# Two attentions: three unread products of 128 rows by 512 columns behind every block of values

## Chip, cores and metric
One core of one Trainium2 chip runs the whole program. The metric is the device time of one execution in microseconds (us), the median of several runs. Lower is better.

## What is computed
Input x has shape (8, 512, 128). Two layers, each an attention and a feed-forward part, each with a residual and a layer norm over the last axis behind it:

```python
x = layernorm(x + attn0(x))   # 16 heads of 8, rotary, causal softmax, output projection
x = layernorm(x + moe(x))     # top 2 of 7 experts, and a shared one
x = layernorm(x + attn1(x))   # 16 heads of 8, rotary, softmax over all keys, no projection
x = layernorm(x + dense(x))   # ternary weights, 128 -> 512 -> 512 -> 512 -> 128
```

The three products of the change feed none of this.

## The kernel before
The function `attention` runs twice, first with the causal mask ("causal attention"), then without ("full attention"). x lies in SBUF in tiles of 128 tokens. Work goes by batch b (8) and, in it, by group of four heads t (4); n = 4b + t counts the 32 groups. A group is cut into units u: 12 in causal attention (three tiles of scores, shortened by the mask, times four heads), 16 in full attention.

The order on each engine is written out by hand. On TensorE the loop over n and u does, in each unit:

- `scores(n, u)`: keys by queries for one head. q and k are split into a high and a low part and stacked as 24 rows of a 32-row quadrant, in fp32r; a 25th row of q subtracts the row's maximum. So the stationary operand has 25 rows by 128 columns. Result to one of three banks ps_s; ScalarE takes the exponential into `prob` (L430).
- `maxima(n+2, u)`: queries by keys, 24 rows, two groups ahead, to one of three banks ps_m; VectorE reduces each to row maxima (L575 causal, L578 full).
- `values`, in some units only (the map `sh.values`): a block j of 128 keys, four heads side by side in the columns of the array, 128x32 each, fp32 (each product is two records in the trace), accumulating in bank ps_o. In causal attention block 0 comes at unit 8, blocks 1, 3 and 2 at units 0, 1 and 4 of the next group; in full attention blocks 0, 1, 2 come at units 6, 10, 14 and block 3 at unit 2 of the next group.
- `job`, in some units: small work through the one bank ps_x (XB = 1), each with a stationary operand of 128x128: `maxT` (maxima transposed, every group), `norm` (outputs transposed for the division, every group), and once per batch `xT`, `k`, `q`, `v`, and in causal attention `yT` and `proj`. A job waits until the job before it has been read out of the bank (semaphores `s_read`): ScalarE reads most, VectorE reads norm and proj.

SyncE (SP) issues the transfers. `stack(b)` copies the high and low parts of k and q of a batch into `kst` and `qst` by 24 DMAs; `max_row(n)` moves the row of maxima of group n into `qst`. Both stand in one queue: in each batch, stack(b+1) is issued between the rows of its second and third groups. The first scores of a group wait for its row. The lines that move a row and wait for it:

```python
for n in range(G):
    if n + 1 < G:
        max_row(n + 1)
    if n % NG == 0 and n // NG + 1 < B:
        stack(n // NG + 1)
```

GpSimd does the rotary arithmetic and hides the masked part of the diagonal blocks (`hide`).

Of the kernel before, what the change touches and what calls it, by code (L numbers as in the profile page):

```python
# [11 lines left out]
P = 128  # L12
# [6 lines left out]
NG = H // HG  # L19
# [110 lines left out]
def after(eng, sem, count):  # L130

    if count > 0:
        eng.wait_ge(sem, count)
# [98 lines left out]
def attention(nc, sems, x, x_dram, ident, maskw, weights, wproj, cos, sin, tag, ahead=None):  # L232
# [4 lines left out]
    U = sh.units  # L237
    G = B * NG
    SB, MB, XB = 3, 3, 1
    START = [("xT", 0), ("k", 0), ("q", 0), ("v", 0), ("xT", 1), ("k", 1), ("q", 1), ("maxT", 0)]  # L240
    END = [("norm", G - 1)] + ([("yT", B - 1), ("proj", B - 1)] if causal else [])
    place = sh.ring(START, END, XB)

    with ExitStack() as ctx:
        def psum(name, shape, dt=F32):
            return ctx.enter_context(nc.psum_tensor(tag + name, shape, dt))

        def sbuf(name, shape, dt=F32):
            return ctx.enter_context(nc.sbuf_tensor(tag + name, shape, dt))
# [3 lines left out]
        kst = [sbuf(f"kst{r}", [P, NG, T], F32R) for r in range(2)]  # L253
# [22 lines left out]
        ps_j = [psum(f"ps_x{i}", [P, T]) for i in range(XB)]  # L276
# [4 lines left out]
        s_made, s_read, s_swap, s_turn, s_hi, s_lo = sems.made, sems.read, sems.swap, sems.turn, sems.hi, sems.lo  # L281
# [3 lines left out]
        def stacked(b):  # L285

            return (b // 2 + 1) * STACK

        with nc.Block() as block:
# [63 lines left out]
            def _(pool):  # L353
# [9 lines left out]
                def hide(n, j):  # L363

                    k, (col, _) = sh.tile_of[j], sh.piece_of[j]
                    pool.wait_ge(s_exp, n * U + (k + 1) * HG)
                    diag = prob[k][:, :, col:col + P]
                    pool.affine_select(out=diag, in_=diag, compare_op=ALU.is_ge, fill=0.0, base=0,  # L368
                                       pattern=[[0, HG], [1, P]], channel_multiplier=-1).then_inc(s_mask, 1)
# [20 lines left out]
            def _(act):  # L390
# [48 lines left out]

                for name, n in START:  # L440
                    read_out(name, n)
# [11 lines left out]

            @block.tensor
            def _(pe):
                def job(name, n):

                    slot, before = place[name, n]
                    ps_x = ps_j[slot]
                    if before is not None:  # L460
                        pe.wait_ge(s_read[before[0]], before[1] + 1)
                    if name == "xT":
                        if causal:
                            pe.wait_ge(s_load[n], 16)
                        for i in range(QT):
                            last = pe.transpose(ps_x[:, P * i:P * i + P], x[:, QT * n + i, :], ident[:, :])
                    elif name in "kq":
                        pe.wait_ge(s_read["xT"], n + 1)
                        last = pe.matmul(ps_x[:, :], weights[name][:, :], xT[:, :], start=True, stop=True)
                    elif name == "v":  # L470
                        for i in range(QT):
                            last = pe.matmul(ps_x[:, P * i:P * i + P], xT[:, P * i:P * i + P], weights["v"][:, :],
                                             start=True, stop=True)
                    elif name == "maxT":
                        pe.wait_ge(s_mx, (n + 1) * U)
                        last = pe.transpose(ps_x[:, 0:P], mx[n % 2][:, :], ident[:, :])
                    elif name == "norm":
                        pe.wait_ge(s_oT, n + 1)
                        for i in range(QT):
                            last = pe.transpose(ps_x[:, P * i:P * i + P], oT[:, P * i:P * i + P], ident[:, :])  # L480
                    elif name == "yT":
                        pe.wait_ge(s_read["norm"], (n + 1) * NG)
                        for i in range(QT):
                            last = pe.transpose(ps_x[:, P * i:P * i + P], y[:, i, :], ident[:, :])
                    else:
                        assert name == "proj"
                        pe.wait_ge(s_read["yT"], n + 1)
                        for i in range(QT):
                            last = pe.matmul(ps_x[:, P * i:P * i + P], yT[:, P * i:P * i + P], wproj[:, :],
                                             start=True, stop=True)  # L490
                    last.then_inc(s_made[name], 1)

                def scores(n, u):

                    b, t = divmod(n, NG)
                    r, (k, i), g = b % 2, divmod(u, HG), n * U + u
                    if u == 0:
                        pe.wait_ge(s_mst, (n + 1) * 16)
                    after(pe, s_exp, g - SB + 1)
                    lo_row, end = QUAD * i, QUAD * i + KROWS + 1  # L500
                    for j, col, w in sh.score[k]:
                        last = pe.matmul(ps_s[g % SB][:, col:col + w], kst[r][lo_row:end, t, P * j:P * j + P],  # L502
                                         qst[r][lo_row:end, t, T - w:T], start=True, stop=True)
                    last.then_inc(s_score, 1)

                def maxima(n, u):

                    b, t = divmod(n, NG)
                    r, (k, i), g = b % 2, divmod(u, HG), n * U + u
                    if u == 0 and t == 0:  # L510
                        pe.wait_ge(s_kst[r], stacked(b))
                        pe.wait_ge(s_qst[r], stacked(b))
                    i = (i + 2) % HG
                    after(pe, s_mx, g - MB + 1)
                    lo_row, end = QUAD * i, QUAD * i + KROWS
                    for j, col, w in sh.maxima[k]:
                        last = pe.matmul(ps_m[g % MB][:, col:col + w], qst[r][lo_row:end, t, P * j:P * j + P],  # L517
                                         kst[r][lo_row:end, t, 0:w], start=True, stop=True)
                    last.then_inc(s_max, 1)

                def values(n, j):

                    b, t = divmod(n, NG)
                    k, (col, w) = sh.tile_of[j], sh.piece_of[j]
                    if causal:
                        pe.wait_ge(s_mask, sh.values_done(n, j))
                    else:
                        pe.wait_ge(s_exp, n * U + (k + 1) * HG)
                    if j == 0:
                        after(pe, s_oT, n)  # L530
                        if t == 0:
                            pe.wait_ge(s_read["v"], b + 1)
                    for i in range(HG):
                        last = pe.matmul(ps_o[VW * i:VW * i + VW, T - w:T], vst[b % 2][:, j, HG * t + i, :],  # L534
                                         prob[k][:, i, col:col + w], start=(j == 0), stop=(j == sh.order[-1]))
                    last.then_inc(s_pv, 1)

                for name, n in START[:-1]:
                    job(name, n)
                for u in range(U):  # L540
                    maxima(0, u)
                for u in range(U):
                    maxima(1, u)
                    if u == 3:
                        job("maxT", 0)
                for n in range(G):
                    for u in range(U):
                        scores(n, u)
                        if n + 2 < G:
                            maxima(n + 2, u)  # L550
                        for back, j in sh.values.get(u, []):
                            if n >= back:
                                values(n - back, j)
                        for name, m in sh.jobs(n, u):
                            job(name, m)
                for j in [j for u in sorted(sh.values) for back, j in sh.values[u] if back]:
                    values(G - 1, j)
                for name, n in END:
                    job(name, n)
# [1457 lines left out]
```

## Time and profile before

| | us |
|---|---|
| median of 3 runs | 1616.12 |
| lowest, highest | 1610.1, 1623.22 |
| the profiled execution | 1627.57 |
| its span, first to last instruction | 1625.9 |
| TensorE busy | 1321.6 |
| VectorE busy | 927.4 |
| ScalarE busy | 795.7 |
| GpSimd busy | 520.5 |

The mean granted clock of TensorE over the span is 0.753 (1 is 2.4 GHz, 0.5 is 1.2 GHz). PE is TensorE's matmul part, PEld its weight loads, DVE VectorE, ACT ScalarE, POOL GpSimd, SP SyncE. Matmul records overlap, since a product goes through the array while the next one starts; so the distance from start to start tells what one costs, and its recorded duration is longer.

### The profile page before, as it was taken

Reading aid. Unit: us, or ns where it says so; the run is one execution under the profiler, and the core shown is the slowest. Engines: PE = TensorE matmul, PEld = TensorE weight load, DVE = VectorE, ACT = ScalarE, POOL = GpSimd, SP = SyncE. Lnnn points to the kernel's source line nnn. Section 1 sums busy time; section 2 is a strip of 40 time slices with the busy share of each in tenths; the row PEclk is TensorE's granted clock in tenths of the full one; section 3 lists DMA queues with packets and bytes.
Section 4 is the critical chain, followed back from the end, with each engine's and each line's share of the span. In section 5 each row is a group of like instructions: output and inputs, shape, how many; then the busy total and the mean of one; then the engine's idle time right before and its main releaser. Section 6 shows DMA issues by size and latency. Waiting matters only on the chain. (4 is left out here: it accounts for less than half of the span.)

```text
span 1625.9 us, 21073 instructions
## 1 busy us (share of the span) xinstructions
PE 1321.6 (81%) x6651; PEld 681.9 (42%) x6651; DVE 927.4 (57%) x2838; ACT 795.7 (49%) x1543; POOL 520.5 (32%) x476
## 2 busy tenths in 40 slices
PE   3678977788898586983589888888888867999997
PEld 1334333333333454761223223233232216888885
DVE  3546665675563774547557777777686513343443
ACT  1234444554444662533146656557565434655653
POOL 3314423551411465654203113113030002554453
PEclk9966576875556698995557778778585557999998
DMA  4212112211200402431321121120220000000000
GB/s 98 35 22 41 19 23 40 40 19 23 40 2 1 127 7 63 109 66 34 80 56 24 17 40 18 23 40 16 26 41 1 1 0 20 1 26 13 13 19 14
DMA packets 55918, 52.77 MB, mean 32 GB/s; under 512 B 8000, under 2 KB 38720, under 8 KB 55824
## 3 DMA queue, kind: packets, MB, share of 16 engines
q1 hardware_dynamic: 51808, 48.33, 15.4%
q0 software_dynamic: 3696, 2.76, 1.3%
q8 instruction: 47, 0.77, 0.2%
q14 instruction: 47, 0.39, 0.1%
q10 hardware_dynamic: 320, 0.52, 0.1%
HBM read 15.74 MB, written 8.06 MB: 15 GB/s over the span
## 5 line engine op out<-in xcount | busy, mean ns | idle before, releaser
L430 ACT ACTIVATE a_prob<-a_ps_s 128x512 f32<-128x512 f32 (+1 forms) x896 | 472.3, 568 | 461.2 <-PE a_ps_s L502 458.9
L578 DVE TENSOR_REDUCE a_mx<-a_ps_m 128x1 f32<-128x512 f32 x512 | 329.3, 684 | 156.0 <-PE a_ps_m L517 154.6
L517 PE MATMUL a_ps_m<-a_kst,a_qst 24*128 24x512 f32 (+3 forms) x1024 | 379.5, 577 | 46.4 <-DMA a_qst<-a_lo_q 36.9
L502 PE MATMUL a_ps_s<-a_qst,a_kst 25*128 25x512 f32 (+3 forms) x1024 | 359.7, 572 | 49.5 <-DMA a_qst<-a_mrow 34.3
L534 PE MATMUL a_ps_o<-a_prob,a_vst 128*32 128x512 f32 (+3 forms) x2048 | 339.6, 749 | 2.2 <-POOL a_prob L368 1.4
L575 DVE CUSTOM_DVE_ANT_0 a_junk<-a_ps_m,maskw 128x384 f32<-128x384 f32 (+3 forms) x512 | 230.1, 487 | 188.0 <-PE a_ps_m L517 186.0
L502 PEld LDWEIGHTS a_ps_s<-a_qst,a_kst 25*128 25x128 f32 x1024 | 158.8, 247 | 404.9 <-ACT a_prob L430 207.2
L517 PEld LDWEIGHTS a_ps_m<-a_kst,a_qst 24*128 24x128 f32 x1024 | 169.8, 246 | 77.9 <-issue 40.5
L368 POOL TENSOR_SCALAR_AFFINE_SELECT a_prob<-a_prob 128x512 f32<-128x512 f32 x128 | 79.7, 635 | 308.7 <-ACT a_prob L430 308.4
L335 POOL TENSOR_TENSOR a_rot_k<-a_rot_k,sin_table 128x512 f32<-128x512 f32 x16 | 20.4, 1272 | 313.4 <-DVE a_rot_k L586 313.4
L480 PE MATMUL a_ps_x<-ident,a_oT 128*128 128x128 f32 x256 | 60.5, 382 | 70.4 <-ACT a_oT L438 48.4
L1676 POOL TENSOR_TENSOR f_hid_lo<-f_gelu_h,f_hid_hi 128x512 fp32r<-128x512 f32 x64 | 83.1, 1299 | 101.8 <-ACT f_hid_hi L1639 101.8
L1714 PE MATMUL f_ps_h<-f_hid_hi,f_h_hi 128*128 128x512 f32 x256 | 103.5, 404 | 4.5 <-POOL f_hid_lo L1676 4.5
L1676 POOL TENSOR_TENSOR f_hid_lo<-f_gated_h,f_hid_hi 128x512 fp32r<-128x512 f32 x32 | 41.4, 1295 | 193.2 <-ACT f_hid_hi L1628 192.5
L1716 PE MATMUL f_ps_h<-f_hid_lo,f_h_hi 128*128 128x512 f32 x256 | 101.4, 396 | 0.0
L1715 PE MATMUL f_ps_h<-f_hid_hi,f_h_lo 128*128 128x512 f32 x256 | 100.7, 393 | 0.0
L534 PEld LDWEIGHTS a_ps_o<-a_prob,a_vst 128*32 128x32 f32 x2048 | 47.2, 127 | 83.3 <-issue 53.4
L480 PEld LDWEIGHTS a_ps_x<-ident,a_oT 128*128 128x128 f32 x256 | 39.5, 191 | 92.7 <-issue 65.8
L1714 PEld LDWEIGHTS f_ps_h<-f_hid_hi,f_h_hi 128*128 128x128 f32 x256 | 48.8, 191 | 16.1 <-POOL f_hid_lo L1676 6.7
L1811 DVE SCALAR_TENSOR_TENSOR f_u<-f_th,f_ps_a 128x512 f32<-128x512 f32 x32 | 21.9, 683 | 56.0 <-ACT f_th L1623 56.0
L1716 PEld LDWEIGHTS f_ps_h<-f_hid_lo,f_h_hi 128*128 128x128 f32 x256 | 48.6, 190 | 11.2
L1715 PEld LDWEIGHTS f_ps_h<-f_hid_hi,f_h_lo 128*128 128x128 f32 x256 | 48.8, 191 | 10.1
(290 smaller groups left out, 1885.3 us busy)
## 6 DMA issues: line engine op xcount, KB each, us to landing
a_kst<-a_hi_k SPq DMA_DIRECT2D x128, 64.0 KB
a_qst<-a_hi_q SPq DMA_DIRECT2D x128, 64.0 KB
f_w<-in_L_ffn_W_dram SPq DMA_DIRECT2D x21, 256.0 KB, 3.5
a_kst<-a_lo_k SPq DMA_DIRECT2D x64, 64.0 KB
a_qst<-a_lo_q SPq DMA_DIRECT2D x64, 64.0 KB
x_tiles<-in_L_attn_x_dram SPq DMA_DIRECT2D x8, 256.0 KB, 4.8
normed_rows_dram<-f_nrm SPq DMA_DIRECT2D x8, 256.0 KB, 2.3
f_hT_hi<-expert_sums_dram SPq DMA_DIRECT2D x4, 512.0 KB, 6.0
```

Source lines behind the costliest of these rows:

```text
L368: pool.affine_select(out=diag, in_=diag, compare_op=ALU.is_ge, fill=0.0, base=0, pattern=[[0, HG], [1, P]], channel_multiplier=-1).then_in ...
L430: act.activation(prob[k][:, i, 0:w], ps_s[g % SB][:, 0:w], ACT.Exp, scale=float(D) ** -0.5)\
L480: last = pe.transpose(ps_x[:, P * i:P * i + P], oT[:, P * i:P * i + P], ident[:, :])
L502: last = pe.matmul(ps_s[g % SB][:, col:col + w], kst[r][lo_row:end, t, P * j:P * j + P], qst[r][lo_row:end, t, T - w:T], start=True, stop= ...
L517: last = pe.matmul(ps_m[g % MB][:, col:col + w], qst[r][lo_row:end, t, P * j:P * j + P], kst[r][lo_row:end, t, 0:w], start=True, stop=True)
L534: last = pe.matmul(ps_o[VW * i:VW * i + VW, T - w:T], vst[b % 2][:, j, HG * t + i, :], prob[k][:, i, col:col + w], start=(j == 0), stop=(j ...
L575: ins = dve.tensor_tensor_reduce(junk[g % MB][:, col:col + w], bank[:, col:col + w], maskw[:, T - w:T], 1.0, -3.0e38, ALU.add, ALU.max, out)
L578: ins = dve.reduce_max(out, bank[:, col:col + w], AX.X)
L1676: pool.tensor_tensor(dst, src[:, :], hi.bitcast(F32), ALU.subtract).then_inc(s_lo, 1)
L1714: pe.matmul(out, w_hi[w][:, k, cols], hi, start=start, stop=False)
L1715: pe.matmul(out, w_lo[w][:, k, cols], hi, start=False, stop=False)
L1716: return pe.matmul(out, w_hi[w][:, k, cols], lo, start=False, stop=stop)
```

## The change
Behind every block of values, also where a group has no values yet, TensorE does three products of a 128x128 piece of `kst` with 512 columns of `kst`, fp32r, into bank ps_x. Nobody reads them. Ahead of each three it waits until the last job in ps_x has been read.

```diff
@@ -237,6 +237,7 @@
     SB, MB, XB = 3, 3, 1
+    WARM = 3
@@ -453,9 +454,20 @@
             @block.tensor
             def _(pe):
+
+                held = [None] * XB
+
+                def warm(r, t):
+
+                    if held[0] is not None:
+                        pe.wait_ge(s_read[held[0][0]], held[0][1] + 1)
+                    for _ in range(WARM):
+                        pe.matmul(ps_j[0][:, :], kst[r][:, t, 0:P], kst[r][:, t, :], start=True, stop=True)
+
                 def job(name, n):
 
                     slot, before = place[name, n]
+                    held[slot] = (name, n)
                     ps_x = ps_j[slot]
@@ -551,6 +563,7 @@
                         for back, j in sh.values.get(u, []):
                             if n >= back:
                                 values(n - back, j)
+                            warm(n // NG % 2, n % NG)
                         for name, m in sh.jobs(n, u):
                             job(name, m)
```

## Rows read from the trace of the kernel before

**Rows 1.** The page: TensorE's busy time, and its granted clock in 40 slices.
```profile
PE 1321.6 (81%) x6651; PEld 681.9 (42%) x6651; DVE 927.4 (57%) x2838; ACT 795.7 (49%) x1543; POOL 520.5 (32%) x476
PEclk9966576875556698995557778778585557999998
```

**Rows 2.** Windows over causal and full attention; the first row names the columns.
```profile
core 0: us, PE busy (x) PEld busy (x) DVE busy (x) ACT busy (x) POOL busy (x), PEclk, DMA share, GB/s
66.81:521.50 454.69, 380.85 (x2358) 169.88 (x2356) 263.67 (x1230) 220.41 (x478) 154.10 (x188) 0.66 0.17 26
...
808.74:1330.80 522.06, 455.20 (x2266) 150.21 (x2266) 349.04 (x750) 303.89 (x598) 75.82 (x60) 0.68 0.16 26
```

**Rows 3.** Windows over single groups: two of full, two of causal attention.
```profile
990.13:1002.67 12.54, 10.86 (x73) 3.63 (x71) 11.26 (x23) 9.67 (x20) 8.10 (x7) 1.00 0.01 2
1257.45:1276.17 18.72, 16.46 (x69) 4.99 (x69) 12.72 (x35) 9.12 (x19) 0.00 (x0) 0.50 0.01 2
232.89:241.98 9.09, 7.49 (x67) 3.51 (x63) 7.97 (x37) 6.84 (x17) 6.20 (x8) 1.00 0.01 2
...
216.45:232.89 16.44, 15.28 (x84) 5.91 (x83) 9.74 (x47) 7.47 (x16) 2.17 (x4) 0.54 0.01 1
```

**Rows 4.** Windows over batches: causal first and last, full fifth and last.
```profile
66.81:127.46 60.65, 50.49 (x269) 22.32 (x271) 31.33 (x139) 26.93 (x59) 14.73 (x20) 0.72 0.20 27
...
470.13:521.50 51.37, 46.71 (x277) 19.90 (x277) 21.14 (x98) 25.82 (x56) 10.27 (x17) 0.57 0.00 1
...
1064.47:1126.81 62.34, 53.83 (x293) 18.59 (x293) 46.97 (x103) 38.65 (x78) 12.62 (x11) 0.75 0.17 27
...
1257.45:1330.80 73.35, 62.74 (x239) 18.06 (x239) 25.97 (x67) 35.75 (x71) 0.00 (x0) 0.50 0.00 1
```

**Rows 5.** Windows in full attention: ahead of a rise, behind it, without one.
```profile
979.30:986.10 6.80, 6.80 (x33) 1.96 (x32) 4.32 (x8) 3.75 (x7) 0.00 (x0) 0.50 0.00 0
986.10:1006.60 20.50, 17.29 (x114) 5.67 (x110) 17.65 (x32) 15.59 (x32) 11.72 (x10) 1.00 0.01 2
1225.00:1305.00 80.00, 70.61 (x288) 21.55 (x288) 43.68 (x96) 38.48 (x77) 0.00 (x0) 0.50 0.00 1
```

**Rows 6.** Two of these windows, products to ps_x alone (PE busy, PEclk, DMA).
```profile
979.30:986.10 6.80, 1.16 (x5) 0.50 0.00 0
...
1225.00:1305.00 80.00, 7.22 (x24) 0.50 0.00 1
```

**Rows 7.** Waits of PE in full attention, longest total first (us, times, longest).
```profile
PE a_ps_x L480 <- ACT a_oT L438: 38.6, 31, 1.3
PE a_ps_s L502 <- ACT a_prob L430: 10.8, 34, 0.7
PE a_ps_x L476 <- DVE a_mx L578: 9.9, 28, 0.5
```

**Rows 8.** Timeline of full attention at full clock (start, us, engine, line).
```profile
1119.05 1.07 PE L534 MATMUL a_ps_o<-a_prob,a_vst 128*32 128x512 f32 x8
...
1120.05 0.49 PE L502 MATMUL a_ps_s<-a_qst,a_kst 25*128 25x512 f32 x1
...
1120.08 0.29 DVE L598 TENSOR_TENSOR a_y<-a_ps_x,a_rden 128x128 f32<-128x128 f32 x1
...
1120.48 1.12 PE L469 MATMUL a_ps_x<-a_xT,heads_q 128*128 128x512 f32 x2
...
1121.54 0.49 PE L502 MATMUL a_ps_s<-a_qst,a_kst 25*128 25x512 f32 x1
```

**Rows 9.** A window over the dense stage.
```profile
1400.00:1600.00 200.00, 200.00 (x900) 163.34 (x899) 90.43 (x237) 113.66 (x171) 99.81 (x77) 1.00 0.05 15
```

**Rows 10.** Timelines of SP and of PE: a stack and the row behind it.
```profile
246.23 5.67 SPq L302 DMA_DIRECT2D a_kst<-a_hi_k  x8
...
263.36 0.56 SPq L314 DMA_DIRECT2D a_qst<-a_mrow  x1
...
271.35 0.79 PE L502 MATMUL a_ps_s<-a_qst,a_kst 25*128 25x512 f32 x1 [6.12 <-DMA a_qst<-a_mrow]
```

## The prediction
> **What bounds the kernel now.** I first read the page's busy shares and its line of granted clock [rows 1]: TensorE is busy 81% of the span, and its clock stands near full only in the expert and dense stages, between 5 and 8 tenths in both attentions. The windows over the stages [rows 2] give the sizes: causal attention 454.69 us at a mean clock of 0.66, full attention 522.06 us at 0.68, together 60% of the span. The clock has two levels, 1.2 and 2.4 GHz, so 0.68 means some 64% of the time at the lower one.
>
> What a level is worth is seen in windows over one group of four heads [rows 3]. In full attention a group takes 12.54 us at clock 1.00 and 18.72 us at 0.50; in causal attention 9.09 us at 1.00, and 16.44 us at 0.54. So at the low level TensorE sets the pace; at the high one it shares it with VectorE, busy 11.26 of 12.54 us.
>
> Then what comes ahead of a rise. From 1225 to 1305 us the clock stays at 0.50 while TensorE is busy 70.61 of 80 us; its longest wait in full attention is 1.3 us [rows 5, 7]. Busy time alone does not raise the clock. What the rows show ahead of the rise at 986.1 is 6.8 us of unbroken work in which jobs with a stationary operand of 128x128 take 1.16 us (17%) beside the values; in the 80 us without a rise such jobs take 7.22 (9%) [rows 6]. Scores and maxima use 24 or 25 of the array's 128 rows, and a values product 32 of its columns; xT, k, q, v and norm use all of it. Every rise that I followed in full attention comes behind a stretch with one of the big jobs, and the last batch, which has none, is cold for all of its 73.35 us [rows 4].
>
> **The change part by part.** It adds 12 products of 128x128 by 512 columns to each group: 4 lumps of 3, 128 lumps in each attention. It removes nothing and adds one wait per lump.
>
> *Price of a lump.* Such products in fp32r run in the dense stage 900 in 200 us, 0.222 us each at full clock, weight loads hidden [rows 9]. Three take 0.67 us. A full-array job in attention pays something on top when the array goes over to another shape: q, two records in fp32, takes from 1120.48 to 1121.54 [rows 8], 1.06 us where four passes of 0.222 make 0.89, so 0.17. A lump stands right behind values, whose own changeover it may share. Bounds 0.67 and 0.84; I take 0.74, nearer the lower end because values also use all rows. Cold, a lump costs about twice that, 1.4.
>
> *The wait.* Ahead of a lump TensorE waits until the last job in the bank has been read. Queued behind it are the next scores and maxima, for which ScalarE and VectorE wait. It bites at one lump per group: behind values of block 0, where norm was the last job. The values end at 1120.05, VectorE's second read of norm at 1120.37 [rows 8]: 0.3 us. In the other lumps the job is two units or more old.
>
> *Clock.* A lump puts some 0.7 us (warm) or 1.4 us (cold) of full-array work behind every block of values, every 3 to 4 us of warm time, which in any such stretch is more than the 1.16 us of jobs that stood ahead of a rise [rows 6]. I therefore expect full attention at 0.97 to 1.00 from its second group on, and causal attention near 0.9, low only around its waits for DMA.
>
> *Full attention.* A batch of 62.34 us at 0.75 is half cold [rows 4]: 31.2/18.72 groups cold, the other 2.33 in 31.2 us, 13.4 us each; a plain warm group is 12.54. I take 12.9, so 32 groups make 413, less 3 for the last two, which have no maxima: 410, a gain of 112. Against it 128 lumps of 0.74 are 95 and 32 waits of 0.3 are 10, less 20 for places where TensorE now waits for VectorE or ScalarE anyway and a lump takes up the wait, plus 3 for a cold start: 88. Net -24.
>
> *Causal attention.* Here a fixed time hides some lumps. SyncE issues the 24 DMAs of a stack from 246.23 to 263.3, then the row of maxima; TensorE sat idle 6.12 us for that row until 271.35 [rows 10]: 25.1 us that no product moves. Six lumps (4.4 us) fall into it and are absorbed. Ten of each batch's 16 are exposed: 7.4, and 0.5 of waits. The group behind the wait takes 16.44 us at 0.54 [rows 3]; at full clock it would be near 9.9 (the 9.09 of the fourth group, and 0.8 for its longer jobs), and as it starts cold I put it at 11.9 without lumps, -4.5. A warm batch of 55.2 us (25.1 + 30.1) becomes 30.1 - 4.5 + 7.9 + 25.1 = 58.6. The first six batches take 344.7 now (60.65 the first; the eight make up the stage), so six of 58.6 are +7. The last two, with few big jobs, take 109.9 at 0.56 to 0.57 (51.37 the last [rows 4]); I put them at 99, -11. Net -4.
>
> *Sum.* -28 on the profiled execution: 1627.57 - 28 = 1600. That execution was 11.5 us above the median and 4 above the slowest of the timed runs. Part is the profile, part the luck of where the clock falls, which the change should take away; I take off about 9 for it: **1590 us**. The expert and dense stages are not touched.
>
> The Trainium skill ("TensorE: Matmul & The Clock Gate", section "HAM oscillation — how this bites in real kernels") ties the clock to idle gaps between bursts and advises keeping the array supplied. By that rule full attention, with no gap over 1.3 us, would be at full clock already and the lumps would be pure cost. The trace disagrees (0.50 for 80 us at 88% busy); the rule's outcome is the first rival.
>
> **The rivals.** *A: the clock does not follow the lumps.* Then each is work at the present mix: 128 lumps at 0.64 x 1.4 + 0.36 x 0.74 = 1.16 make 149 us, and some 80 exposed in causal attention 93: about 1865. For it: the clock's cause is only inferred. Against it: the rises behind jobs of the same kind. The skill's rule just named would give this. Chance 0.07.
>
> *B: the lump is dearer than it looks (slower).* If the 128-column weight load, 163.34 us for 899 or 0.18 us each in the dense stage [rows 9], is not hidden as it is there, each product costs 0.40 and a lump with its changeover some 1.25. Exposed are 128 + 70 lumps. The gain of 28 is gone at 0.74 + 28/198 = 0.88; at 1.25 the change costs 101 - 28 = 73: 1663. For it: operand and weights come from one tile and each lump stands between two shapes. Against it: in the dense stage loads hide one by one. Chance 0.11 for a time over 1632.
>
> *C: it cancels.* A lump at 0.84 gives +20 on my sum, or the group behind the DMA wait stays cold and pays its lumps at 1.4: +20. About 1612. Chance 0.25.
>
> *D: more is absorbed.* VectorE's slack in full attention hides lumps and the clock is full in causal attention too: -25 more, 1565. It belongs to my side; with the forecast itself 0.57.
>
> **How the numbers follow.** Two timings of this kernel within 1% cannot be told from no change. Faster by over 1% (under 1600) is forecast and D, 0.57; within 1% C, 0.25; slower A and B, 0.18. The range runs from below D, 1550, to 1640, past C and into B; left out are A, most of B and a little below: about 0.2.
>
> **What the profile will show.** Right: granted clock above 0.95 in full attention, the last batch no longer at 0.50, groups of about 15.5 us and almost alike; lumps starting 0.22 to 0.24 us apart; the wait for the row of maxima shorter than 6 us but the 25 us from the first DMA of a stack unchanged; the third group of a causal batch below 16 us. Wrong: a clock as before (A), more than 0.3 us between products or 0.9 us from a lump to the next scores (B), a causal group behind the DMA wait still at 0.5 (C). The forecast is most sensitive to the lump: 0.1 us on it is 20 us of time.

## The result and the profile after

The change makes the kernel slower: median 1688.54 us (1679.31 to 1691.43, 4 runs) against 1619.67 us (4 runs of before, three of them those of the table above), ratio 1.0425 with a 95% interval of 1.0351 to 1.0499. The forecast was 1590 us, range 1550 to 1640. The profiled execution took 1679.31 us, span 1677.6 us, which is 51.7 us over the span of before.

The page of the kernel after, its line of engine shares and its granted clock in 40 slices, against [rows 1]:

```profile
PE 1355.9 (81%) x7419; PEld 743.0 (44%) x7419; DVE 927.6 (55%) x2838; ACT 797.2 (48%) x1543; POOL 521.2 (31%) x476
PEclk9999999979978698895599999999999977999999
```

The clock line does what was forecast: nearly all nines in both attentions. TensorE has 768 more records and is not idler than before. The windows, against [rows 2] (causal, full) and [rows 3] (a fourth group of full attention, a fourth and a third of causal):

```profile
core 0: us, PE busy (x) PEld busy (x) DVE busy (x) ACT busy (x) POOL busy (x), PEclk, DMA share, GB/s
66.73:548.43 481.70, 411.19 (x2726) 198.62 (x2729) 265.71 (x1230) 220.68 (x477) 154.07 (x187) 0.92 0.16 24
836.89:1383.43 546.54, 459.70 (x2650) 182.33 (x2650) 349.12 (x750) 304.78 (x599) 75.95 (x60) 0.95 0.16 25
956.21:972.86 16.65, 13.79 (x83) 5.27 (x83) 11.81 (x23) 9.70 (x20) 8.84 (x8) 1.00 0.01 1
231.58:244.75 13.17, 11.21 (x83) 5.31 (x83) 8.54 (x37) 7.00 (x16) 7.19 (x8) 1.00 0.00 1
...
215.80:231.58 15.78, 14.32 (x96) 6.25 (x95) 9.64 (x47) 7.40 (x16) 2.17 (x4) 0.90 0.01 2
```

Read them by pairs. The clock of full attention went from 0.68 to 0.95, that of causal attention from 0.66 to 0.92; yet both became longer. Full attention runs from its first to its last exponential in 546.5 us instead of 522.1. The causal windows of before and after do not end at the same point, so I compare first to last exponential there too: 481.7 us against 453.0 (the start of the last one was at 519.82 before). So +24.5 and +28.7. The fast group shows why: at clock 1.00 both times, 16.65 us instead of 12.54, and in causal attention 13.17 instead of 9.09. Four lumps, with the waits ahead of them, cost 4.1 us a group, where my sum had 2.7.

Two lumps of full attention in the timeline (start, us, engine, line), to be set beside [rows 8]:

```profile
940.59 1.07 PE L546 MATMUL a_ps_o<-a_prob,a_vst 128*32 128x512 f32 x8
...
941.59 0.97 PE L465 MATMUL a_ps_x<-a_kst 128*128 128x512 f32 x3
942.48 0.50 PE L514 MATMUL a_ps_s<-a_qst,a_kst 25*128 25x512 f32 x1
...
945.24 1.06 PE L546 MATMUL a_ps_o<-a_prob,a_vst 128*32 128x512 f32 x8
...
946.26 0.29 DVE L611 TENSOR_TENSOR a_y<-a_ps_x,a_rden 128x128 f32<-128x128 f32 x1
...
946.61 0.97 PE L465 MATMUL a_ps_x<-a_kst 128*128 128x512 f32 x3 [0.31 <-DVE a_y L611]
947.51 0.49 PE L514 MATMUL a_ps_s<-a_qst,a_kst 25*128 25x512 f32 x1
```

From the start of a lump to the next scores it is 0.89 to 0.90 us (941.59 to 942.48, 946.61 to 947.51), and values still take their 1.00 us before it. So the price of a lump is 0.90 us, on top of values that cost what they did before. The second lump starts 1.37 us after its values instead of 1.00: the wait for norm.

The waits of TensorE in full attention, against [rows 7], and below them one of causal attention:

```profile
PE a_ps_x L492 <- ACT a_oT L439: 39.0, 31, 1.3
PE a_ps_x L488 <- DVE a_mx L591: 20.1, 30, 0.7
PE a_ps_s L514 <- ACT a_prob L431: 16.6, 35, 0.7
PE a_ps_x L465 <- DVE a_y L611: 7.0, 23, 0.3
...
PE a_ps_s L514 <- DMA a_qst<-a_mrow: 14.1, 6, 4.2
```

Two more lines of the kernel before belong beside them, the first of full, the second of causal attention:

```profile
PE a_ps_m L517 <- DVE a_mx L578: 6.0, 16, 1.3
...
PE a_ps_s L502 <- DMA a_qst<-a_mrow: 34.3, 7, 7.1
```

Of the waits of full attention that I had counted on to take up 20 us, one went away: the 6.0 us for VectorE's maxima ahead of ps_m are no longer among the waits. The one for the outputs stays (38.6 to 39.0), that of maxT for VectorE's maxima doubled (9.9 to 20.1), that for ScalarE's exponentials grew (10.8 to 16.6), and the new ones ahead of the lumps come on top. So on balance nothing was absorbed. In causal attention the wait for the row behind the stack of DMAs fell, from 34.3 to 14.1 us, and the stack itself kept its time (timelines of SP and of PE, against [rows 10]):

```profile
250.66 5.67 SPq L303 DMA_DIRECT2D a_kst<-a_hi_k  x8
...
276.17 0.50 PE L514 MATMUL a_ps_s<-a_qst,a_kst 25*128 25x512 f32 x1 [2.60 <-DMA a_qst<-a_mrow]
```

That is 25.5 us from first DMA to first scores, 25.1 before.

### The profile page after: what moved, and what is told of

Same layout as the page of the kernel before. It is cut to its first block and busy times, and to the rows that moved or that the text cites. A ratio compares the mean times of both kernels' runs of the same rounds, so it can differ in the third digit from the quotient of the medians.

```text
span 1677.6 us, 22609 instructions
## 1 busy us (share of the span) xinstructions
PE 1355.9 (81%) x7419; PEld 743.0 (44%) x7419; DVE 927.6 (55%) x2838; ACT 797.2 (48%) x1543; POOL 521.2 (31%) x476
## 5 line engine op out<-in xcount | busy, mean ns | idle before, releaser
L529 PE MATMUL a_ps_m<-a_kst,a_qst 24*128 24x512 f32 (+3 forms) x1024 | 292.5, 461 | 39.2 <-DMA a_qst<-a_lo_q 36.9
L514 PE MATMUL a_ps_s<-a_qst,a_kst 25*128 25x512 f32 (+3 forms) x1024 | 276.1, 447 | 35.9 <-ACT a_prob L431 21.5
L465 PE MATMUL a_ps_x<-a_kst 128*128 128x512 f32 x768 | 269.4, 462 | 28.1 <-DVE a_y L611 15.0
L546 PE MATMUL a_ps_o<-a_prob,a_vst 128*32 128x512 f32 (+3 forms) x2048 | 257.1, 577 | 1.4 <-POOL a_prob L369 0.7
L465 PEld LDWEIGHTS a_ps_x<-a_kst 128*128 128x128 f32 x768 | 136.4, 206 | 246.1 <-DVE a_y L611 80.3
L514 PEld LDWEIGHTS a_ps_s<-a_qst,a_kst 25*128 25x128 f32 x1024 | 121.7, 191 | 199.6 <-issue 109.9
L529 PEld LDWEIGHTS a_ps_m<-a_kst,a_qst 24*128 24x128 f32 x1024 | 131.1, 196 | 58.9 <-issue 40.5
L492 PE MATMUL a_ps_x<-ident,a_oT 128*128 128x128 f32 x256 | 43.5, 296 | 74.8 <-ACT a_oT L439 52.4
L492 PEld LDWEIGHTS a_ps_x<-ident,a_oT 128*128 128x128 f32 x256 | 28.4, 146 | 91.2 <-issue 64.8
L546 PEld LDWEIGHTS a_ps_o<-a_prob,a_vst 128*32 128x32 f32 x2048 | 41.5, 111 | 60.4 <-issue 35.1
```

Of the source, the lines that this page charges most:

```text
L465: pe.matmul(ps_j[0][:, :], kst[r][:, t, 0:P], kst[r][:, t, :], start=True, stop=True)
```

## The experiments

All ratios are to the kernel before, timed beside them.

**One product in place of three.** Which part of a lump is fixed, and what the clock does with fewer products.

```diff
-    WARM = 3
+    WARM = 1
```

> One product in place of three behind every block of values. Theory (the price of three is 0.90 us and nothing of it is absorbed, the clock follows the work of the whole array): a lump of one costs 0.43 us, the wait for norm stays at 0.37 us a group, the clock in full attention stays at about 0.9. Full attention: 32 groups of 12.7 us warm, and 55 us of lumps, 12 of waits, 15 to 20 for the cold share, near 493 us against 522 before; causal attention about 10 us under before. Together near 1590 us, ratio 0.975 to 0.99. Rival (the time is lost to the wait for the bank, not to the products): nearly as slow as with three, ratio over 1.02. Rival (three are needed for the clock): clock near 0.75 and ratio near 1.02.

Measured: 1658.28 us, ratio 1.0212 (1.0119 to 1.0305). Windows over an all-warm fourth group and over full attention, and a lump in the timeline:

```profile
949.82:964.64 14.82, 12.26 (x75) 4.26 (x75) 11.81 (x23) 9.70 (x20) 8.54 (x7) 1.00 0.01 2
829.18:1360.81 531.63, 450.71 (x2394) 158.24 (x2394) 350.33 (x750) 304.89 (x598) 75.90 (x60) 0.83 0.15 25
```
```profile
951.86 0.50 PE L465 MATMUL a_ps_x<-a_kst 128*128 128x512 f32 x1
952.29 0.50 PE L514 MATMUL a_ps_s<-a_qst,a_kst 25*128 25x512 f32 x1
```

The price of the lump was right, 0.43 us, but the total was not: full attention took 531.6 and not 493, and causal attention 472.0, above the 453.0 of before and not 10 us below. With one product the clock of full attention is only 0.83, and the warm group is 14.82, not 12.7 plus 2.1. Against three products the group differs by 1.83 us for eight products, 0.23 each; with one, a lump plus its share of waiting still costs (14.82 - 12.54)/4 = 0.57. Both rivals were partly right: some of the price does not depend on the number of products, and with fewer of them more groups fall to the low clock.

**The waits without the products.** The share of the wait for the bank.

```diff
-    WARM = 3
+    WARM = 0
```

> The change's waits for the bank behind every block of values, with no products. Theory (the products with their changeover are what costs): at most 0.37 us in each warm group of full attention and nothing in a cold one, so between 0 and 8 us, ratio 0.995 to 1.01, clocks as before. Rival (the waits for the bank are what costs): near the change's ratio, 1.02 or more.

Measured: 1636.01 us, ratio 1.0107 (0.9996 to 1.0219), clock 0.757 as before. The total cannot be told from no change. The warm fourth group can be read more sharply:

```profile
930.46:943.52 13.06, 10.73 (x71) 3.57 (x71) 11.39 (x23) 9.70 (x20) 8.09 (x7) 1.00 0.01 2
```

13.06 us against 12.54: the waits cost 0.52 us in a warm group, where I had put 0.3 in the prediction and at most 0.37 before this run. What is left of the change's 4.11 is 3.59, four times 0.90, the price that the timeline shows.

The waits of this group, first before, then in this run, show that the wait of maxT grows with the waits for the bank alone:

```profile
PE a_ps_x L476 <- DVE a_mx L578: 0.2, 1, 0.2
```
```profile
PE a_ps_x L488 <- DVE a_mx L591: 0.7, 1, 0.7
```

In the two other groups of full attention that this run has at full clock it is 0.4 us; with the change it is 0.7 in every group. So most of the growth, if not all, needs no products.

**Thin products.** Is it the work over the whole array, or being busy, that moves the clock? Same places, same number of columns, 24 rows of kst in place of 128.

```diff
-pe.matmul(ps_j[0][:, :], kst[r][:, t, 0:P], kst[r][:, t, :], start=True, stop=True)
+pe.matmul(ps_j[0][:, :], kst[r][0:KROWS, t, 0:P], kst[r][0:KROWS, t, :], start=True, stop=True)
```

> Three products as in the change, at the same places and of the same length, but of 24 of the array's 128 rows. Theory (the clock follows work over the whole array): mean clock over the span stays below 0.8, full attention between 0.65 and 0.75, and the time is over 1740 us, as each lump is paid at the low level. Rival (the clock follows busy time of the engine or the number of products): clock as with the change, 0.98 in full attention, and a time at or below the change's 1688 us.

Measured: 1894.69 us, ratio 1.1694 (1.1597 to 1.179), clock 0.683 over the span. Full attention:

```profile
953.31:1599.65 646.34, 586.63 (x2650) 232.75 (x2650) 352.00 (x750) 305.55 (x598) 75.83 (x60) 0.62 0.13 21
```

TensorE has exactly as many records as with the change (2650) and is busy 586.63 of 646.34 us, 91%, at a clock of 0.62. So a busy TensorE and this number of products do not by themselves raise the clock; the clock went up only where the added products took 128 rows by 128 columns. This also is what rival A would have looked like.

Two things limit the reading. First, the thin products do not stand alone: they start together with the scores behind them, so the lumps are not of the same shape in time.

```profile
1299.98 0.79 PE L465 MATMUL a_ps_x<-a_kst 24*128 24x512 f32 x1
1299.99 0.79 PE L514 MATMUL a_ps_s<-a_qst,a_kst 25*128 25x512 f32 x1
```

Second, what it is about the 128x128 product is not separated. A block of values takes all 128 rows with 32 columns for each of four heads, and the records of the four heads start within 0.03 us of each other. Yet in the kernel before such blocks (PE busy with ps_o, then PEclk) filled much of a stretch without any rise:

```profile
1225.00:1305.00 80.00, 32.89 (x136) 0.50 0.00 1
```

**Full attention alone, causal attention alone.**

```diff
-    WARM = 3
+    WARM = 0 if causal else 3      # in the second kernel: 3 if causal else 0
-                    if held[0] is not None:
+                    if WARM and held[0] is not None:
```

> The change's three products in full attention alone. Theory (both attentions lose on their own, full +24 us and causal +28 by the two profiles): 1640 to 1650 us against 1620, ratio 1.01 to 1.02, causal attention as before at a clock of 0.66. Rival (the loss is all in causal attention, and the 24 us of full attention are the luck of its clock before): ratio 0.995 to 1.005.

> The change's three products in causal attention alone. Theory (the two attentions add up; ten of a batch's sixteen lumps are paid at 0.89 us and six fall into the wait for the stack): causal attention 480 to 486 us against 453 before, full attention as before at 0.66 to 0.70, wait for the row behind the stack 0 to 3 us a batch; ratio 1.015 to 1.03. Rival (lumps in causal attention are mostly absorbed, and the loss comes from the stage behind): causal attention below 465 us.

Measured: full alone 1643.9 us, ratio 1.0109 (1.0026 to 1.0192); causal alone 1675.92 us, ratio 1.0439 (1.0315 to 1.0562). Windows over causal and full attention, first of full alone, then of causal alone:

```profile
66.69:522.16 455.47, 385.26 (x2338) 171.18 (x2340) 263.94 (x1230) 220.23 (x477) 153.54 (x187) 0.67 0.17 26
813.25:1355.81 542.56, 455.94 (x2650) 182.13 (x2650) 349.26 (x750) 304.74 (x598) 75.97 (x60) 0.96 0.15 25
```
```profile
66.60:564.11 497.51, 426.75 (x2726) 205.29 (x2729) 265.69 (x1230) 220.74 (x477) 154.09 (x187) 0.88 0.16 24
853.66:1386.35 532.69, 466.99 (x2266) 153.07 (x2266) 349.50 (x750) 303.89 (x599) 75.84 (x60) 0.66 0.16 25
```

Each attention loses on its own, causal attention more. Full alone came out as expected, causal alone did not: 1.015 to 1.03 and 480 to 486 us were expected. But its causal code is the same as the change's, and took 497.5 us here and 481.7 there, at a clock of 0.88 and 0.92: where the clock falls moves one attention by 16 us. Full attention, whose code is here that of before, took 532.7 us instead of 522.1, so the +24.5 above has some 10 us of such luck in it either way. The two ratios fit the whole change within their intervals; the split between the attentions is not known better than that.

**Four products ahead of norm's wait.** Products where TensorE waits anyway.

```diff
-                            warm(n // NG % 2, n % NG)
+    # in job(), behind the wait for the bank, ahead of the wait for the data:
+                    if name == "norm" and fill is not None:
+                        warm(*fill)          # WARM = 4
```

> No products behind values; four full-array products per group ahead of the wait of the job norm, where TensorE waits 1.25 us for ScalarE in full attention. Theory (work of the whole array raises the clock wherever it stands, and products in a wait cost nothing): four take 1.1 us, hidden in full attention; clock there 0.8 to 0.9, full attention 455 to 485 us against 522; causal attention between -15 and +10 us, as the wait there is 0.5 to 1.15 us. Ratio 0.96 to 0.98. Rival (the wait is not free, since what releases it is itself late): ratio 1.00 or more.

Measured: 1571.75 us, ratio 0.9708 (0.9628 to 0.9788). An all-warm fourth group, full and causal attention, and the place in the timeline:

```profile
889.02:901.50 12.48, 12.03 (x77) 4.32 (x75) 11.26 (x23) 9.67 (x20) 8.11 (x7) 1.00 0.00 1
783.69:1272.48 488.79, 452.75 (x2390) 168.63 (x2390) 346.55 (x750) 304.64 (x599) 76.15 (x60) 0.79 0.17 28
66.63:492.31 425.68, 344.81 (x2466) 174.38 (x2468) 262.49 (x1230) 218.43 (x477) 153.71 (x187) 0.84 0.18 28
```
```profile
891.56 1.20 PE L462 MATMUL a_ps_x<-a_kst 128*128 128x512 f32 x4
892.74 0.66 PE L491 MATMUL a_ps_x<-ident,a_oT 128*128 128x128 f32 x4
```

The group takes 12.48 us with four more full-array products in it, against 12.54 without. They fill the 1.25 us wait for the outputs, which is gone from this group's waits. The clock rises to 0.79 and 0.84, less than with the change, but in such a group nothing is paid for it. Full attention took 488.8 us, a little above the 455 to 485 expected; the causal part won more than expected (-27 us, not -15 to +10).

**Eight in place of four.** What a product costs that no longer fits.

```diff
-    WARM = 4
+    WARM = 8
```

> Eight products ahead of norm's wait in place of four. Theory (beyond the wait a product costs 0.23 us and there is no second changeover): the four that no longer fit add 0.75 to 0.95 us to a warm group of full attention, 12.47 to 13.2 or 13.4, without the 0.33 us of a lump behind values; the clock of full attention goes from 0.79 to about 0.9. Total 1575 to 1600 us. Rival (products in front of a late release delay it too, or share its cost): a warm group as at four, or above 13.8.

Measured: 1617.1 us, ratio 1.0025 (0.9968 to 1.0083), above the 1575 to 1600 expected. The warm group:

```profile
920.83:934.00 13.17, 12.69 (x81) 5.17 (x79) 11.26 (x23) 9.67 (x21) 8.16 (x7) 1.00 0.01 2
```

0.69 us over the group with four, so the price held in full attention (four products of 0.23 less some slack). But the clock of full attention reached 0.81, not 0.9, and full attention took 510.5 us; causal attention took 451.7, 26 more than with four, for which the expectation had no term. Twice as many products in the same place raised the clock by only 0.02.

**Two more ahead of maxT.**

```diff
+                    if name == "maxT" and fill is not None:
+                        warm(*fill, WARM_T)  # 2, beside 4 ahead of norm
```

> Four products ahead of norm and two ahead of maxT, in both attentions. Theory: two take 0.47 us in a wait of 0.2 to 0.66 us, so 0.1 to 0.3 us a group exposed; the clock of full attention goes from 0.79 to 0.95 or so and its time from 489 to between 420 and 440 us; causal attention within 10 us. 1510 to 1540 us. Rival (two more are paid in full and the clock's gaps lie elsewhere): over 1565.

Measured: 1581.56 us, ratio 0.9818 (0.975 to 0.9887): a miss, the rival was right. The clock of full attention went to 0.83 only, for 483.6 us, and causal attention took 442.0, 16 more than with four ahead of norm alone.

**24 products ahead of the stack's row.** With four ahead of norm the third group of a causal batch, behind the DMA wait, was still slow (first row). In this run the array is kept busy during that wait (second row).

```diff
+                    if causal and n % NG == 2 and n + NG < G:
+                        pe.wait_ge(s_read[held[0][0]], held[0][1] + 1)
+                        warm(n // NG % 2, n % NG, 24)
                     for u in range(U):
                         scores(n, u)
```

> Four products ahead of norm, and 24 more in causal attention ahead of the first scores of each batch's third group, where TensorE waits 6 to 9 us for the row behind the stack of DMAs. Theory (that wait is fixed by the queue, and the group behind it is cold only because the array idled): they take 5.8 us inside the wait, the third group goes from 16.5 us at 0.58 to 10.5 to 12 us at 0.9 or more, seven times: 30 to 40 us less than with four ahead of norm alone, 1530 to 1545 us. Rival (the group is slow for another reason, or the clock falls again before it starts): 1565 to 1580.

```profile
319.23:336.36 17.13, 15.97 (x88) 6.95 (x87) 9.74 (x47) 7.47 (x16) 2.17 (x4) 0.57 0.01 1
```
```profile
315.09:326.37 11.28, 10.15 (x87) 4.69 (x87) 9.85 (x47) 7.21 (x16) 2.18 (x4) 1.00 0.00 1
```
```profile
308.89 5.74 PE L462 MATMUL a_ps_x<-a_kst 128*128 128x512 f32 x24 [0.96 <-ACT a_vst L410]
```

Measured: 1546.82 us, ratio 0.9585 (0.9517 to 0.9653), the lowest median of all versions. The same group took 11.28 us at 1.00 instead of 17.13 at 0.57. In two of the seven batches the low clock came back in that group all the same (17.85 at 0.52, 15.29 at 0.67; the profiled execution, 1565.6 us, is the slowest of the four). The gain, 25 us between the medians, is under the 30 to 40 expected. The 24 products both end the idle wait and add work of the 128x128 kind; the run does not tell which of the two keeps the clock up.

**Lumps behind values in light groups only**, on top of that.

```diff
+                            light = n % NG == 1 or n // NG >= B - 2 and n % NG >= 2 or n // NG == B - 1
+                            if not causal and (u == 14 and (light or n % NG == 0) or u == 10 and light):
+                                pe.wait_ge(s_read[held[0][0]], held[0][1] + 1)
+                                warm(n // NG % 2, n % NG, 2)   # in the other kernel: 1
```

> As the run with 24 products ahead of the stack's row, and in full attention two products behind values at units 10 and 14, only in groups without a big job, and at unit 14 of each batch's first group. With four ahead of norm the low clock lay between unit 9 or 14 of a light group and unit 4 of the next, so the second groups took 19.3 us at 0.59. Theory (a lump costs 0.33 + 0.23 each less the wait, 0.66 us here, and holds the clock up there): second groups 13.5 to 14.5 us at 0.95 or more, full attention 425 to 450 us against 489 to 494; median 1485 to 1510 us, ratio about 0.925. Rival (the lumps cost what they win, as in the change): full attention 480 us or more, ratio 0.95 to 0.96.

> The same with one product in place of two in each of these lumps. Theory: 0.43 us each; if one is enough for the clock, 8 us less than with two, else the second groups stay partly at the low level and it is 10 to 30 us more.

Measured: two products 1549.67 us, ratio 0.9599 (0.9492 to 0.9705); one product 1554.28 us, 0.9678 (0.9612 to 0.9744), the two not to be told apart, nor from the run without these lumps. A miss of 40 us; the rival was right. Full attention with two:

```profile
766.40:1252.20 485.80, 446.25 (x2456) 168.02 (x2456) 345.92 (x750) 304.71 (x598) 76.21 (x60) 0.87 0.17 28
```

The clock rose from 0.78 to 0.87, and the time of full attention fell from 494.0 to only 485.8: the lumps cost what they win, as in the change. The second groups of a batch still took 17.3 to 19.3 us in six of the eight.

## Why the prediction was wrong

**The clock step was right.** Full attention was to be at 0.97 to 1.00 and is at 0.95; causal near 0.9 and is at 0.92. The thin products show that it takes products of 128 rows by 128 columns and not only a busy engine, though not which property of them. Rival A is out.

**The price of a lump was mis-sized.** I took 0.74 between bounds of 0.67 and 0.84, "nearer the lower end because values also use all rows". The lump measures 0.90, outside the bounds. Its first two products start 0.34 us apart where the next are 0.24, and from the last product to the scores it is 0.33. The first 0.10 looks like a weight load that is not hidden, since the lump's first load starts with its first product, but no run isolates that. The values ahead keep their 1.00 us, so nothing is shared with them. It is rival B by its point of decision (0.88), though not by its mechanism: inside the lump the loads are mostly hidden, at 0.23 us a product, and the fixed 0.2 us at the edges, with nothing shared, is what was short. In full attention: 128 x 0.16 = 20 us. (B's own terms, three products of 0.40 and 0.17 for the changeover, add up to 1.37 and not to its 1.25; they would give 1687 us, and that this is the measured time is coincidence, as no product costs 0.40.)

**The waits.** 0.3 us a group became 0.52 with the products taken out: 32 x 0.22 = 7 us.

**"Less 20 for places where TensorE now waits": this step failed altogether.** One wait of 6.0 us was taken up in full attention, and others grew by more (9.9 to 20.1, 10.8 to 16.6), so the 20 us were not there. The wait for the outputs shows why a lump does not shorten it: it is 1.2 to 1.3 us in every group, before and after, at either clock. ScalarE does not copy the outputs as soon as the values are done; in its order the exponential of the next scores comes first, and these scores stand behind the lump, at 942.48. A lump of 0.9 us delays them, and with them the exponential, the copy and norm:

```profile
943.02 0.60 ACT L431 ACTIVATE a_prob<-a_ps_s 128x512 f32<-128x512 f32 x1 [1.58 <-PE a_ps_s L514]
943.51 0.59 ACT L439 ACTIVATE a_oT<-a_ps_o 128x512 f32<-128x512 f32 x1
...
944.25 0.63 PE L492 MATMUL a_ps_x<-ident,a_oT 128*128 128x128 f32 x4 [1.26 <-ACT a_oT L439]
```

The wait of maxT grew for the most part for another reason, the waits for the bank: without products it is already 0.4 to 0.7 us at full clock, where it was 0.2.

These three are 47 of the 48 us by which full attention was missed (546.5 against 498). The steps that separate them are the group without products (13.06), with one (14.82) and with three (16.65). That the sum closes so well is partly luck, since two more terms were off and cancel. This is a batch of the kernel after with all four groups at full clock:

```profile
906.60:972.86 66.26, 55.48 (x340) 22.36 (x340) 46.84 (x103) 38.76 (x77) 12.65 (x11) 1.00 0.18 25
```

Eight of these, less the 3 us for missing maxima, are 527. The other 19 us are groups that were at the low clock in part, where the sum had 3. In return the plain warm group of 12.9 us was too dear: 66.26 less four times 4.11 leaves 12.46 a group, an estimate from these rows, and 32 x 0.44 is 14 us.

**Causal attention.** Six lumps in the fixed time of the stack cost nothing, as forecast: the wait for the row fell from 34.3 to 14.1 us and the 25 us stayed. The third group came out at 15.8 to 15.9 us at 0.89 to 0.90 in four of the seven batches with a stack (forecast "below 16"), the fourth at 13.17 where my terms make 12.2. But rival C was right in places: in the fifth batch the third group took 21.39 us, as low in clock as before.

```profile
336.82:358.21 21.39, 20.23 (x96) 8.94 (x95) 9.74 (x47) 7.47 (x17) 2.18 (x4) 0.57 0.00 1
```

The first six batches took 363 us against 352 forecast. Ten lumps of 0.90 in place of 0.74 are 6 x 10 x 0.16 = 10 of these 11, and the slow third group another 5, so something else was less than forecast; what, is open. The last two took 118.6 against 99. There I had no sum, only a guess of what a group without big jobs would be; a warm first group took 12.9 us, and a third group was back at the low clock (18.19 at 0.56). How much of the 20 us is price and how much the luck of the clock is open: the same causal code differed by 16 us between two profiled executions.

**From the profile to the median.** I took off 9 us for a luck of the clock that the change would remove. The profiled execution of after is 9 us below its median, so this was a guess in the wrong direction, and it makes up 18 us of the 98 between 1590 and 1688.5. Full attention is 48 of them, causal attention 31.

## What to carry to other kernels

Work that keeps the clock up is free only inside a wait whose end does not depend on TensorE, or just ahead of one that it would sit out anyway; put there, it gave -3% and -4%, and behind the values, where TensorE is the pace, +4%. For a wait on an engine that TensorE feeds, it matters on which side of the product that this engine takes next the new work stands: ahead of it, it only moves the wait (a lump ahead of the scores); between it and the wait, it fills it (the four ahead of norm). Price an inserted product between its neighbours, with the first weight load and both changeovers, and not by its spacing in a long run of its own kind.

## What the runs showed of the hardware

At the same count of products in full attention, the granted clock was 0.62 with 24-row products, TensorE 91% busy, and 0.95 with 128-row ones, TensorE 84% busy. The 0.90 us lump and the 0.43 us single product against a spacing of 0.23 put the price of going from narrow products to wide ones and back at an estimated 0.2 us.

The Trainium skill ("TensorE: Matmul & The Clock Gate", section "HAM oscillation — how this bites in real kernels") speaks of idle gaps. What happened behind the stack fits it: with the wait filled, the group behind it went from 0.57 to 1.00, though the filling was itself 128x128 work. The thin products do not fit it: 0.62 in full attention with no wait of TensorE over 1.0 us.
